# Attention with a value product for every two groups: the product moved behind the turned scores of its slot

## The reference

```python
q = _heads(jnp.concatenate([ssm_states, hidden_states], axis=-1) @ Wq, H)   # 32 heads of 16
k = _heads(hidden_states @ Wk, HK)                                          # 8 heads, each for 4 of q
ssm_k = _heads(ssm_states @ Wsk, HK)                                        # v, ssm_v in the same way
kcat = jnp.concatenate([rep(ssm_k), rep(k)], axis=2)
scores = jnp.einsum('bhqd,bhkd->bhqk', q, kcat) / np.sqrt(D) + bias         # alibi
scores = jnp.where(mask, scores, -jnp.inf)                                  # a key counts for 64 positions
o = jnp.einsum('bhqk,bhkd->bhqd', jax.nn.softmax(scores, axis=-1), vcat)
x = x + jnp.tanh(g_xattn[0]) * (o @ Wo)                                     # then the experts
```

## Time and profile before

| | us |
|---|---|
| median of three runs | 885.44 |
| the profiled execution | 887.48 |
| its span, first to last instruction | 885.3 |
| PE busy | 865.7 (98%) |
| DVE busy | 541.4 (61%) |
| POOL busy | 510.1 (58%) |
| ACT busy | 403.6 (46%) |

### The profile page before, as it was taken

How to read it: one execution, slowest core, us unless ns; L and a number is a source line. 1 busy time by engine, 2 the same in 40 slices (tenths; PEclk the granted TensorE clock), 3 DMA queues, 4 the chain that set the end, 5 groups by cost and what they waited for, 6 DMA issues and landing times.

```text
span 885.3 us, 17385 instructions
## 1 busy us (share of the span) xinstructions
PE 865.7 (98%) x6662; PEld 755.6 (85%) x6662; DVE 541.4 (61%) x983; ACT 403.6 (46%) x812; POOL 510.1 (58%) x526
## 2 busy tenths in 40 slices
PE   8899999999999999899999999999999999999998
PEld 8889999999999998787878867888888888888886
DVE  7675666667667667452336748466565565565567
ACT  6655555455546455356134243443443444444431
POOL 3761434434343414143499994456788888788741
PEclk9999999999999999899999999999999999999999
DMA  8677586767778679530101244402202021121046
GB/s 272 171 152 181 148 202 183 189 193 186 204 176 201 166 192 247 138 99 24 48 25 48 70 156 158 167 25 71 72 25 96 25 71 35 62 72 48 1 140 240
DMA packets 77947, 110.17 MB, mean 124 GB/s; under 512 B 7329, under 2 KB 49058, under 8 KB 76834
## 3 DMA queue, kind: packets, MB, share of 16 engines
q1 hardware_dynamic: 75656, 108.04, 43.2%
q10 hardware_dynamic: 2210, 1.03, 0.5%
HBM read 71.76 MB, written 32.05 MB: 117 GB/s over the span
## 4 chain that ended last, share of the span: by engine, by line
PE 86%; DMA 4%; POOL 3%; DVE 2%; SPq 2%; issue 2%; ACT 1%; POOLq 0%; DVEq 0%
PE ps_scores L2198 20%; PE ps_proj L1822 15%; PE ps_scoresT L2198 10%; PE ps_scoresT L1959 6%; PE ps_proj L1811 6%; PE ps_o L1973 6%; PE ps_scores L1932 5%; PE ps_proj L2198 5%; PE ps_proj L1880 4%; PE ps_scores L1822 4%; PE ps_scoresT L1822 3%; DMA xnT_lo<-xT_kept 2%; DMA k_kept<-kT_lo 1%; SPq L612 1%; DMA ctx_turned<-in_ctx 1%
## 5 line engine op out<-in xcount | busy, mean ns | idle before, releaser
L1110 ACT ACTIVATE probsT<-ps_scoresT 128x512 f32<-128x512 f32 (+1 forms) x256 | 138.5, 544 | 157.1 <-PE ps_scoresT L1959 152.7
L1461 DVE TENSOR_REDUCE neg_max<-ps_scores 128x2 f32<-128x384 f32 (+1 forms) x256 | 131.8, 517 | 116.8 <-PE ps_scores L1932 116.1
L1328 ACT ACTIVATE part_sums<-ps_scores 128x512 f32<-128x512 f32 x96 | 57.4, 598 | 133.4 <-PE ps_scores L2198 130.4
L1959 PE MATMUL ps_scoresT<-q_stack,k_stack 116*128 116x256 f32 x448 | 106.2, 308 | 0.0
L827 POOL TENSOR_TENSOR o_normal<-o_blocks,inv_sums 128x256 f32<-128x256 f32 x32 | 19.9, 622 | 149.4 <-DVE inv_sums L1482 149.4
L1932 PE MATMUL ps_scores<-k_stack,q_stack 114*128 114x192 f32 (+1 forms) x512 | 95.1, 268 | 3.1 <-DMA q_stack<-qT_hi 2.0
L1932 PEld LDWEIGHTS ps_scores<-k_stack,q_stack 114*128 114x128 f32 x512 | 83.7, 191 | 10.3 <-DMA q_stack<-qT_hi 2.4
L973 POOL TENSOR_TENSOR w_expert_lo<-w_sums,w_expert_hi 128x256 fp32r<-128x256 f32 x64 | 63.9, 1009 | 45.4 <-ACT w_expert_hi L1251 45.4
L985 POOL TENSOR_TENSOR big<-big,basis 128x512 f32<-128x512 f32 x56 | 77.5, 1402 | 14.9 <-DVE basis L1761 14.9
L1959 PEld LDWEIGHTS ps_scoresT<-q_stack,k_stack 116*128 116x128 f32 x448 | 70.8, 191 | 3.8
L1752 DVE TENSOR_TENSOR basis<-part_sums,silu_gate 128x512 f32<-128x512 f32 x32 | 24.2, 756 | 67.3 <-ACT silu_gate L1336 67.3
(11 more groups left out here) (311 smaller groups left out, 2498.1 us busy)
## 6 DMA issues: line engine op xcount, KB each, us to landing
k_stack<-k_kept SPq DMA_DIRECT2D x64, 192.0 KB, 4.5
big<-coeff_rows SPq DMA_DIRECT2D x8, 1024.0 KB, 4.6
q_stack<-q_kept SPq DMA_DIRECT2D x40, 192.0 KB, 4.1
q_kept<-qT_hi SPq DMA_DIRECT2D x10, 512.0 KB
x_rows<-in_x SPq DMA_DIRECT2D x9, 512.0 KB, 6.5
k_kept<-kT_hi SPq DMA_DIRECT2D x16, 256.0 KB
x_kept<-x_rows SPq DMA_DIRECT2D x16, 256.0 KB, 2.6
w_raw<-in_L_ffn_w_gate SPq DMA_DIRECT2D x16, 256.0 KB, 2.9
```

The costliest lines, as they stand in the source:

```text
L1110: act.activation(PT[:, g % 2, 2 * j:2 * j + blocks].rearrange("p h f r w -> p (h f r w)"), ST[:, n % 2, 0:blocks].rearrange("p h n -> p (h ...
L1328: act.activation(TP[:, u % 2, j, :], src[:, u % 2, :], ACT.Copy).then_inc(taken, 1)
L1461: dve.tensor_reduce(NM[:, g // 2 % 2, g % 2, 2 * i:2 * i + 2], SA[:, n % 2, :, 0:keys], AX.X, ALU.max, negate=True).then_inc(max_done, 1)
L1959: ins = pe.matmul(ST[:, n % 2, v, :], KS[0:ROWS, g, j + v, 1 - v].rearrange("p w s -> p (w s)"), QS[0:ROWS, g, j + v].rearrange("p f r w - ...
```

## The change

In each slot the value product is now issued behind the turned maxima and the turned scores; nothing else is changed.

```diff
@@ -2080,14 +2080,14 @@
             if n < END:
                 scores(n)
-            p = pair_due(n, PV)
-            if p is not None:
-                times_v(p)
             p = pair_due(n, NM_TURN)
             if p is not None:
                 turn_max(p)
             if LAG <= n < END + LAG:
                 scores_turned(n - LAG)
+            p = pair_due(n, PV)
+            if p is not None:
+                times_v(p)
```

## The result

The change measured 889.8 us (median of 22 executions) against 887.66 for the kernel before on the same chip (22): a ratio of 1.0025 with an interval of 1.0013 to 1.0037, that is +2.2 us, between +1.2 and +3.3. The direction and the place were as forecast, but it cost more than twice the +0.9 us, and 889.8 lies above the range's end of 889.0. The interval leaves out 1.0000, so this is a small loss and not, as forecast, a change that reads as none. Single executions of either kernel spread by 7 us, so one of them tells nothing of 2 us.

A forecast was written before the change was run, and what follows sets the result against it. PE, busy 98% of the span, was taken to bound the kernel by its own instruction list. Seams +0.3 and product 30 +0.6 made +0.9 us on a median of 885.44: 886.3 us, range 883.8 to 889.0.

The forecast's parts named there:

- the forecast's sum: Whole kernel: +0.3 us for the seams and +0.6 for product 30, together +0.9 us on 885.44.
- the clock: Rival at product 30: one idle piece of 2.1 us halves PE's clock, costing some 3.4 us; 7 in 100.
- ACT's earlier start: Step 2, at each product: ACT's exponentials start 0.9 us earlier, worth 0 because nobody on PE waited for them.
- turned maxima never meet a product: In the slots: maxima stand in 9 + 8p, products in 26 + 8p, so that half of the change does nothing.
- Step 1, the seams: Seams between matmuls around 28 steady products: 2.51 us against 2.50, +0.3 us in all, bounds -2.2 and +1.7.
- Step 3, product 30: At product 30, its ready first half is held up behind waiting turned scores: +0.6 us, bounds +0.5 and +0.8.
- pass the waiting matmul: Other case at product 30: a queue letting the ready product go first would make the step -0.3 us instead.
- the hold-up: At product 30: PE's 0.97 us of work before the wait is no longer hidden in it; the step is +0.6 us.
- The late maxima: Rival at turned scores, 1.76 us earlier: maxima's DMA landing beyond 8.7 us; at 10 us, 9 us in all; 4 in 100.

The follow-up runs named there:

- quiet copy: The changed order of PE on the kernel before with SP's router loads of the kept activations issued one to three slots earlier; 0.9976 of before, 884.74 us.
- quiet base: Kernel before, PE and ACT order kept, with SP's router loads of the kept activations issued one to three slots earlier; 0.995 of before, 883.0 us.
- last kernel above: Old PE order with the earlier router loads, plus ACT's first two silu in slot 266 and DVE's first silu-up product two slots later; 0.9954 of before, 883.79 us.
- control: The kernel before, unchanged, run again against itself; 0.9992 (0.9972 to 1.0012).

## Why the prediction was wrong

**The step that failed is the forecast's sum: it put the clock at nothing, and it stood on a base that was 2.2 us too low.** 889.8 lies 3.5 us above the predicted 886.3. Of these, 2.2 are the base and 1.3 are the change, which cost 2.2 where the sum had 0.9. The two steps that the sum did have were nearly right in the traces (+0.57 for +0.3, +0.73 for +0.6); the remaining 0.9 is what the sum had left out, as far as medians of this spread can tell.

**The direction** was right, and so was the reading that ACT's earlier start is worth nothing: at product 13 the exponentials start 1.66 us behind the scores (209.51 to 211.17) instead of 2.50 (208.21 to 210.71), 0.84 earlier where I had said 0.9, and no wait of PE got shorter by it. That turned maxima never meet a product held too.

**Step 1, the seams: right in kind, mis-sized by a hundredth.** I put them at 2.51 against 2.50; the traces say 0.02 each, 0.57 us for 28 where I had 0.3. Turned scores to product was 0.35 (0.36 forecast), scores behind a product 0.30 (0.28 forecast, 0.31 my upper bound): a scores pair inherits the late second weight load in full, as the row behind transposes had it.

**Step 3, product 30: right, +0.7 for +0.6.** The passage is 0.73 longer in the kernel with only this swap, at full clock. The turned scores waited 2.16, where I had said 2.1. The product did not pass the waiting matmul: in the trace after, nothing starts on PE between 401.41 and 403.95, though the product's first half was ready. That agrees with the Trainium skill, page "TensorE: Matmul & The Clock Gate", section "Architectural detail: the array is 16× 32×32, not 1× 128×128", by which PE's queue pulls weight loads ahead.

**The clock, left out of the sum.** I had named it as a rival with 7 chances in 100, arguing that the idle piece was half as long as that before the one drop in the trace. That argument was wrong. With the swap and ACT's wait, the clock fell at product 30 in two of three profiled executions (the change and its quiet copy). It never did so in five with the old order or the product's halves apart (idle pieces of 1.3 to 1.5 us) or in two with the idle time filled (0.86). The price I had wrong in the other direction: 3.4 us if it fell as long as at 356 us; the fall lasted 3.4 us here and cost 1.6 us of time.

What it costs on average is an estimate. The mean granted clock of the change, 0.9955, against the three sets of the kernel before, 0.9963 to 0.9969, gives 0.7 to 1.2 us of 887. With 0.57 and 0.73 that makes 2.0 to 2.5, and 2.2 was measured (1.2 to 3.3). But 1.3 for the seams and the hold-up alone lies within that interval too: that the clock fell behind this wait is in the traces; how much of the 2.2 us it makes on average is not shown. A forecast had to carry this as a term: its chance times its price, since executions mix.

**The base was thin.** I put the sum on 885.44, a median of three; 22 executions give 887.66. With that base my +0.9 would have read 888.6, and the range would have held 889.8, but by its width and not by its terms. One program's executions differ by up to 7 us here, and I took the three for its level.

**The late maxima** cost the change nothing in the execution profiled. But my argument that waits before the change exclude a landing beyond 10.4 us was too strong: it came from one execution. The quiet base with the old order showed one:

```profile
PE ps_scoresT L1959 <- DMA q_stack<-max_rows: 1.5, 1, 1.5
```

The last kernel above, which has the early loads as well, showed another of 0.3 us, and no profiled execution with the old loads showed any. Whether the earlier loads delay this DMA, and whether the wait comes more often with the swap, stays open.

**Also open:** why the clock fell in the profiled executions of the change and of its quiet copy, and not in that of the kernel with only product 30 swapped, behind the same wait of 2.16.

## What to carry to other kernels

Moving a ready instruction behind one that waits costs the work that used to hide in the wait; look for the one place in a list of many where the order matters, and price that place, not the average one. A longer idle piece of PE also brings a chance of half clock behind it: carry it in the sum as chance times price. Take the level of a noisy kernel from many executions, not from three. And before arguing over 2 us, take away the largest varying wait (here the loads' late issue, 4 us and the half clock behind it), which was worth more than the change that it hid.

## What the hardware showed unasked

- The longer PE had been idle, the oftener its clock fell. From 30 to 430 us the profiled executions of all kernels here have 25 idle pieces of PE of over 1.2 us. Behind the eight of 2.4 to 4.3 us, all near 356 us, it fell every time. Behind the seven of 2.0 to 2.2 us it fell five times: at product 30 in the change and its quiet copy, near 356 us in the change, at 90 us in the last kernel above, and near 370 us in the kernel with the turned scores between the halves. The two without a fall are product 30 in the kernel with only that one swapped, and 409 us in the last kernel. Behind the ten of 1.3 to 1.5 us it fell once, at 37 us in the quiet base.
- Each fall lasted 3.4 us, but 6.8 behind the three longest pieces (4.1 to 4.3 us); the kernel before and its control, one program, had 6.8 behind 4.2 us and 3.4 behind 2.4.
